# Expert stage's head, the end of attention and the order of FFN's last chunks: work moved between stages, engines and places in their queues

## The chip, the cores and the metric

The kernel runs on one core of a Trainium2 chip, as one program in one launch. The metric is the device time of an execution in microseconds. The kernel before took 1101.15 us (median of 3 runs, 1100.53 to 1102.22). Engines: PE is TensorE (PEld its weight loads), DVE is VectorE, ACT is ScalarE, POOL is GpSimd, SP is SyncE, which issues transfers.

## The reference

Two transformer layers over x of 2 x 1024 tokens with 128 features, all in float32:

```
x = layernorm(x + attention_16_heads(x))
x = layernorm(x + x + 0.5 * (silu(h @ w1 + b1) @ w2 + b2))   # h: x normalised; w1, w2 dequantised
x = layernorm(x + attention_1(x))                            # scores over all 128 features
n = x * rsqrt(mean(x * x) + 1e-8) * norm_weight
p = sigmoid(n @ router_w.T); the two largest of 8, divided by their sum + 1e-6, are the gates
moe = sum over 8 experts: gate_e * (relu(n @ ew1[e] + eb1[e]) @ ew2[e] + eb2[e])
x = layernorm(x + shared_ffn(n) + moe)                       # shared_ffn: the same form, gate 1
```

The inner residual of FFN is its own (the first `x +` belongs to the layer, the second to the FFN). All 8 experts are computed for all tokens.

## The kernel before, in words

There are four stages, and each is a block: no engine enters the next one before all have left the last. `attend_heads` is the first attention (to 717 us), `quantised_ffn` follows (to 760), then `attend_once` (to 851.7) and `mix_experts` (to the end). The 2048 tokens are 16 tiles of 128 (`T`), or 4 chunks (`CK`, `CHUNKS`) of 512 columns. Chunks 0 and 1 are the early ones, 2 and 3 the late ones (`LATE` = 2). Every product that must be exact is three matmuls: operands are split into a high part, rounded to fp32r, and a low part, which is the rest, and hi*lo, lo*hi and hi*hi are added up in a PSUM bank.

Within a stage each engine has its own queue, written out by hand as a Python function per engine; it is worked off in order. Semaphores tie the queues together (`wait_ge`, `then_inc`).

**FFN.** VectorE's queue is at L891-905. `enter` (L851) puts a chunk's normalised tokens in place of X, `leave` (L864) adds the second product of a chunk and sums for the output's layernorm, `finish` (L881) scales the chunk. `leave` waits for `finish` of the chunk before, since there is one set of statistics for all chunks. ScalarE's `out_root` (L823) takes the root between them.

**Second attention, last step.** In step `STEPS` nothing is left but the products with V (`times_v`), four groups. For each, VectorE inverts the denominator (L1229), ScalarE scales the group (L1179) and VectorE puts the output together (L1233), which frees one of the two PSUM banks. Between them stand, for the early chunks, the layernorm's normalising `normalise_tokens` (L1840-1849, at kt 1 and 3, L1238), the turning of chunk 0's tokens on TensorE (L1127), ScalarE's scaling and rounding of it (L1183, L1185), VectorE's low part (L1241) and GpSimd's `normalise_input` for chunks 0 and 1 (L1017, L1852).

**Expert stage.** `over_ffns` (L1328) runs nine FFNs: `ffn(0)` is the shared one, `ffn(1)` to `ffn(8)` are experts 0 to 7, six of them in a hardware loop. An FFN n has 16 tiles (c, f), four chunks by four parts of the hidden layer. TensorE takes turns: `first_product(n, c, f)` (L1414) into one of two banks `bank_h`, then `second_product` of the chunk before (L1432). ScalarE's `rectify` (L1535) empties `bank_h`; `lead` (L1548, L1627) makes the high part on ScalarE (on VectorE for f = 1 and 3 from expert 0 on), GpSimd the low part (L1382; VectorE's `rest`, L1634, for f = 3 from expert 0 on). VectorE's `take` and `add` (L1640, L1651) multiply by the gates and add to `y_sum`. `split_weights` (L1513 on ScalarE, L1620 on VectorE) splits the next expert's weights; `first_product(n, 0, 0)` waits for it (`w_lo_ready`).

The head of that stage is this. TensorE multiplies the late chunks by the output weights (`times_wo`), turns chunk 1's tokens between them (L1490-1493), and in `ffn(0)` turns chunk 2 and 3 after the tiles of chunk 0 and 1; it multiplies by the router after chunk 1 (`ROUTE_AT` = 1, L1486) and turns the gates after chunk 3 (`GATES_AT` = 3). VectorE adds and sums chunks 2 and 3, normalises both, fills `gates[0]` with ones (L1614), then scales and subtracts both (L1615-1618); in `ffn(0)` it chooses the gates (`choose_gates`, L1705), after that makes the low parts of expert 0's weights, and then takes chunks 0 and 1 of the shared FFN. ScalarE's high parts of chunks 2 and 3 (`take_hi`) stand after the last tile of chunk 0 and 1, its sigmoid after chunk 1. GpSimd fills `y_sum` first (L1372), and after `ffn(0)` it has `normalise_input` for chunks 2 and 3. The gates go to memory and back (SyncE, L1350, L1346), and only after them SyncE loads expert 1's weights (L1353).

```python
for c in range(LATE, CHUNKS):        # FFN, VectorE, L896-905
    normalise_ffn(nc, dve, X, fq, c)
leave(0)
finish(0)
enter(2)
enter(3)
for c in range(1, CHUNKS):
    leave(c)
    finish(c)
```

Of the kernel before, what the change touches and what calls it, by code (L numbers as in the profile page):

```python
# [20 lines left out]
P = 128  # L21
CH = 512
# [659 lines left out]
def quantised_ffn(nc, a, persist):  # L682
# [8 lines left out]
    with ExitStack() as ctx:  # L691
# [9 lines left out]
        out_stats, out_mv = sb("ln_out_stats", [P, 4, 6]), sb("ln_out_mean_var", [P, 4, 2])  # L701
        out_std, out_rstd = sb("ln_out_std", [P, 4]), sb("ln_out_rstd", [P, 4])
# [102 lines left out]
        def _(act):  # L805
# [17 lines left out]
            def out_root(c):  # L823
                act.wait_ge(out_moments, c + 1)
                nc.scalar.activation(out_std[:], out_mv[:, :, 1], ACT.Sqrt, bias=eps[:, 2:3]).then_inc(out_rooted, 1)
# [18 lines left out]
        def _(dve):  # L844
# [19 lines left out]
            def leave(c):  # L864
                dve.wait_ge(b2_added, c + 1)
                if c:
                    dve.wait_ge(out_done, c)
                for j in range(4):
                    dve.wait_ge(z_filled, c + 1 + (j if c == CHUNKS - 1 else 0))
                    add_z(c, j)  # L870
                    if j:
                        dve.wait_ge(z_added, 4 * c + j)
                        nc.vector.bn_stats(out_stats[:, j - 1, :], X[:, 4 * c + j - 1, :])
                dve.wait_ge(z_added, 4 * c + 4)
                nc.vector.bn_stats(out_stats[:, 3, :], X[:, 4 * c + 3, :]).then_inc(out_summed, 1)
                dve.wait_ge(out_summed, c + 1)
                for j in range(4):
                    last = nc.vector.bn_aggr(out_mv[:, j, :], out_stats[:, j, :])
                last.then_inc(out_moments, 1)

            def finish(c):  # L881
                dve.wait_ge(out_rooted, c + 1)
                nc.vector.reciprocal(out_rstd[:], out_std[:]).then_inc(out_inverted, 1)
                dve.wait_ge(out_inverted, c + 1)
                for j in range(4):
                    t = 4 * c + j
                    last = nc.vector.tensor_scalar(X[:, t, :], X[:, t, :], out_mv[:, j, 0:1], out_rstd[:, j:j + 1],
# [52 lines left out]
def attend_once(nc, a, persist):  # L940
# [10 lines left out]
    with ExitStack() as ctx:  # L951
# [56 lines left out]
        def _(pool):  # L1008
# [8 lines left out]
            for c in range(EARLY):  # L1017
                normalise_input(nc, pool, X, ln, c)
# [10 lines left out]
        def _(pe):  # L1029
# [97 lines left out]
            def turn_tokens(c):  # L1127

                pe.wait_ge(exp_done, TB * STEPS)
                pe.wait_ge(ln["n_ready"], c + 1)  # L1130
                for j in range(4):
                    last = nc.tensor.transpose(bank_a[c][:, j * P:(j + 1) * P], persist["n_tok"][:, 4 * c + j, :], ident[:])
                last.then_inc(ln["n_turned"], 1)

            for n in range(AHEAD):
                max_scores(n)
            for step in range(STEPS + 1):
                for kt in range(TB):
# [9 lines left out]
                    if step == STEPS and kt == TB - 3:  # L1148
                        turn_tokens(0)

        @block.scalar
        def _(act):
# [16 lines left out]
            for step in range(STEPS + 1):  # L1169
                for kt in range(TB):  # L1170
# [10 lines left out]
                    if step == STEPS and kt == TB - 3:  # L1181
# [731 lines left out]
```

## Time and profile before

| | |
|---|---|
| median of 3 runs | 1101.15 us |
| the profiled execution: its own time / its span | 1102.37 / 1100.6 us |
| TensorE busy, matmuls | 1040.3 us, 95% of the span |
| VectorE busy | 842.6 us, 77% |
| ScalarE busy | 646.9 us, 59% |
| GpSimd busy | 693.1 us, 63% |
| mean granted TensorE clock | 0.972 |
| chain that ended last | PE 15%, DVE 4%, POOL 1%, ACT 1%, issue 1% |

The span is the time from the first to the last instruction; 1.8 us of the execution's own time lie around it. A granted clock of 1.00 is 2.4 GHz, 0.50 is 1.2 GHz; a value between is a stretch with both. A line of a group gives the busy time, and behind it the idle time of the engine just before these instructions and what ended it. A busy TensorE counts matmuls at whichever clock they ran.

### The profile page before, as it was taken

What the parts mean: (1) busy time and instruction counts of PE and PEld (TensorE: products, weight loads), DVE (VectorE), ACT (ScalarE), POOL (GpSimd) and SP (SyncE); (2) the same over time, 40 slices, a digit from 0 to 9 for tenths busy, and PEclk for the clock granted to TensorE, in tenths of its full rate; (3) what the DMA queues carried; (4) which work ended last, traced back from release to release, by engine and by line L of the source; (5) the groups of instructions that cost most, each with busy time, mean ns of one, the idle gap of its engine ahead of it and who ended that gap; (6) DMA issues with size and microseconds to landing.
All of it is one profiled execution on the core that took longest, in us unless ns stands there. A gap on an engine that the chain in (4) does not pass through costs nothing. (4 is left out here: it accounts for less than half of the span.)

```text
span 1100.6 us, 25309 instructions
## 1 busy us (share of the span) xinstructions
PE 1040.3 (95%) x7983; PEld 858.3 (78%) x7983; DVE 842.6 (77%) x1685; ACT 646.9 (59%) x1311; POOL 693.1 (63%) x671
## 2 busy tenths in 40 slices
PE   5899999999999999999999999887998799999996
PEld 4678888888888888888888888655686677777774
DVE  5877877877877877877877877646765589898896
ACT  4555655655655555555555555664344577666774
POOL 4166876876876876876876877511233377777772
PEclk9989999999999999999999999998899799999998
DMA  6243543543543543543543543110000012212111
GB/s 126 49 93 84 104 95 84 105 94 84 106 94 85 106 93 84 106 93 84 107 92 84 108 92 79 45 31 1 0 1 2 18 61 81 72 57 76 58 39 38
DMA packets 57040, 80.08 MB, mean 73 GB/s; under 512 B 25956, under 2 KB 38048, under 8 KB 55968
## 3 DMA queue, kind: packets, MB, share of 16 engines
q1 hardware_dynamic: 54792, 78.97, 31.4%
q10 hardware_dynamic: 2208, 0.59, 0.3%
q8 instruction: 24, 0.39, 0.1%
q14 instruction: 16, 0.13, 0.0%
HBM read 19.43 MB, written 1.11 MB: 19 GB/s over the span
## 5 line engine op out<-in xcount | busy, mean ns | idle before, releaser
L666 POOL TENSOR_TENSOR probs_lo<-probs 128x512 f16<-128x512 f32 x384 | 419.0, 1105 | 199.6 <-ACT probs L470 197.8
L511 DVE TENSOR_REDUCE maxes<-bank_m 128x1 f32<-128x512 f32 x512 | 353.0, 690 | 138.5 <-PE bank_m L301 134.1
L470 ACT ACTIVATE probs<-bank_s 128x512 f32<-128x512 f32 x512 | 297.4, 607 | 264.9 <-PE bank_s L389 264.3
L382 PE MATMUL bank_s<-qa,ka 128*128 128x512 f32 x512 | 226.6, 442 | 7.3 <-ACT probs L470 3.4
L301 PE MATMUL bank_m<-ka,qa 128*128 128x512 f32 x512 | 207.5, 405 | 2.4 <-DMA ka<-tk_lo 2.4
L389 PE MATMUL bank_s<-qb,kb 65*128 65x512 f32 x512 | 206.5, 403 | 1.1 <-DMA qb<-negmax 1.1
L324 PE MATMUL bank_o<-v_now,probs 128*128 128x129 f16 x2048 | 201.9, 221 | 0.3 <-ACT o_parts L436 0.2
L1382 POOL TENSOR_TENSOR hidden_lo<-rectified,hidden_hi 128x512 fp32r<-128x512 f32 x112 | 156.3, 1414 | 67.1 <-ACT hidden_hi L1554 56.9
L324 PEld LDWEIGHTS bank_o<-v_now,probs 128*128 128x128 bf16 x2048 | 176.2, 98 | 21.3 <-issue 20.5
L320 PE MATMUL bank_o<-v_now,probs_lo 128*128 128x65 f16 x2048 | 185.8, 193 | 0.0
L301 PEld LDWEIGHTS bank_m<-ka,qa 128*128 128x128 f32 x512 | 158.7, 310 | 29.1 <-issue 2.6
L320 PEld LDWEIGHTS bank_o<-v_now,probs_lo 128*128 128x128 f16 x2048 | 174.0, 98 | 0.0
L1546 ACT ACTIVATE rectified<-bank_h,e_bias_now 128x512 f32<-128x512 f32 x144 | 99.2, 689 | 60.1 <-PE bank_h L1430 35.6
L382 PEld LDWEIGHTS bank_s<-qa,ka 128*128 128x128 f32 x512 | 97.4, 190 | 41.1 <-ACT probs L470 30.6
L389 PEld LDWEIGHTS bank_s<-qb,kb 65*128 65x128 f32 x512 | 98.0, 191 | 10.3 <-DMA qb<-negmax 1.4
L588 DVE TENSOR_TENSOR probs_lo<-probs 128x512 f16<-128x512 f32 x128 | 102.0, 797 | 3.8 <-ACT probs L470 3.8
L436 ACT ACTIVATE o_parts<-bank_o,rden 128x129 f32<-128x129 f32 x256 | 79.8, 367 | 2.5 <-DVE rden L523 1.4
L1632 DVE CAST hidden_hi<-rectified 128x512 fp32r<-128x512 f32 x64 | 53.0, 828 | 22.5 <-ACT rectified L1546 22.5
L1654 DVE TENSOR_TENSOR y_sum<-y_sum,y_gated 128x512 f32<-128x512 f32 x36 | 52.3, 1452 | 0.1
L1554 ACT CAST hidden_hi<-rectified 128x512 fp32r<-128x512 f32 x80 | 49.0, 613 | 2.6 <-PE bank_y L1447 2.2
L1004 POOL TENSOR_TENSOR probs_lo<-probs 128x512 f16<-128x512 f32 x16 | 17.1, 1073 | 43.6 <-ACT probs L1174 43.6
L641 POOL TENSOR_TENSOR o_pair<-o_parts 128x256 f32<-128x256 f32 x64 | 41.0, 640 | 4.3 <-ACT o_parts L436 4.3
(269 smaller groups left out, 1686.4 us busy)
## 6 DMA issues: line engine op xcount, KB each, us to landing
qa<-tq_hi SPq DMA_DIRECT2D x64, 256.0 KB, 4.1
v_now<-arena SPq DMA_DIRECT2D x32, 260.0 KB, 2.3
ka<-tk_hi SPq DMA_DIRECT2D x32, 256.0 KB, 3.0
ka<-tk_lo SPq DMA_DIRECT2D x32, 256.0 KB, 5.1
kb<-tk_hi SPq DMA_DIRECT2D x32, 256.0 KB, 5.1
qb<-tq_lo SPq DMA_DIRECT2D x32, 256.0 KB, 5.3
gates_on_all<-gate_rows SPq DMA_DIRECT2D x8, 1024.0 KB, 4.7
e_raw<-in_L_ffn_ew_dram SPq DMA_DIRECT2D x16, 256.0 KB, 3.1
```

The lines of the kernel that those rows point to most:

```text
L301: nc.tensor.matmul(bank_m[j % 2][:], qs, ka[h][:, half * CH:(half + 1) * CH], start=True, stop=True).then_inc(m_filled, 1)
L320: low = lambda: nc.tensor.matmul(acc[:, 0:E + 1], probs_lo[:, s % 2, kt, qs], v[:, kt, 0:E + 1], start=False, stop=False, skip_group_check ...
L324: last = nc.tensor.matmul(acc[:, 0:2 * E + 1], hi_of[:, kt, qs, 1], v[:, kt, 0:2 * E + 1], start=(kt == 0), stop=(kt == UNITS - 1))
L382: nc.tensor.matmul(bank_s[u % 2][:], ka[h][:, ks], qa[h][:, qs], start=True, stop=False)
L389: nc.tensor.matmul(bank_s[u % 2][:], kb[h][0:E + 1, ks], qb[h][0:E + 1, qs], start=False, stop=True).then_inc(s_filled, 1)
L436: nc.scalar.activation(out, src[:, 0:P + 1], ACT.Copy, scale=rden[:, qt:qt + 1]).then_inc(o_taken, 1)
L470: nc.scalar.activation(probs[:, c, u, :], bank_s[u % 2][:], ACT.Exp, scale=SCALE).then_inc(exp_done, 1)
L511: nc.vector.tensor_reduce(maxes[:, j // 2, j % 2:j % 2 + 1], bank_m[j % 2][:], AX.X, ALU.max).then_inc(m_reduced, 1)
L588: nc.vector.tensor_tensor(probs_lo[:, c, u, :], p, hi, ALU.subtract).then_inc(lo_dve, 1)
L666: nc.gpsimd.tensor_tensor(probs_lo[:, c, u, :], p, hi, ALU.subtract).then_inc(lo_pool, 1)
L1382: nc.gpsimd.tensor_tensor(h_lo[:, f, :], r[:, f, :], h_hi[:, f, :].bitcast(F32), ALU.subtract).then_inc(lo_pool, 1)
L1546: nc.scalar.activation(r[:, f, :], bank_h[f % 2][:], ACT.Relu, bias=b1_now[:, half, f:f + 1]).then_inc(rectified, 1)
```

## The change

- FFN: statistics of the output's layernorm get a place per chunk; VectorE's order becomes enter 2, enter 3, (leave, finish) 0, (leave, finish) 1, leave 2, leave 3, finish 2, finish 3.
- Second attention: the early chunks' tokens are normalised after the second and the fourth group (kt 3 and 7); turning, scaling and splitting chunk 0 and GpSimd's two `normalise_input` leave the stage.
- Expert stage: both early chunks are turned there, between the products with the output weights; ScalarE scales and rounds them, GpSimd makes their low parts. GpSimd fills `gates[0]` with ones in place of VectorE, and `y_sum` after the tiles of chunk 0.
- VectorE adds, sums and normalises chunk 2, then chunk 3.
- ScalarE's high parts of chunk 2 and 3 come after tiles (1, 1) and (2, 0); router and sigmoid after tile (2, 1).
- VectorE makes the low parts of expert 0's weights ahead of the choice of gates. The gates are turned after chunk 0 of expert 0 (`GATES_AT` = (1, 0): FFN 1, chunk 0), so FFNs 1 and 2 are taken out of the hardware loop.
- `normalise_input` of chunks 0 to 3 stands after chunk 0 and 3 of FFN 1, chunk 2 of FFN 2 and chunk 1 of FFN 7.

```diff
@@ quantised_ffn, VectorE
             def leave(c):
                 dve.wait_ge(b2_added, c + 1)
-                if c:
-                    dve.wait_ge(out_done, c)
...
-            leave(0)
-            finish(0)
-            enter(2)
-            enter(3)
-            for c in range(1, CHUNKS):
+            for c in range(LATE, CHUNKS):
+                enter(c)
+            for c in range(LATE):
                 leave(c)
+                finish(c)
+            for c in range(LATE, CHUNKS):
+                leave(c)
+            for c in range(LATE, CHUNKS):
                 finish(c)
@@ attend_once: GpSimd, TensorE, ScalarE, VectorE
-            for c in range(EARLY):
-                normalise_input(nc, pool, X, ln, c)
...
-                    if step == STEPS and kt == TB - 3:
-                        turn_tokens(0)
...
-                    if step == STEPS and kt == TB - 3:
-                        act.wait_ge(ln["n_turned"], 1)
-                        nc.scalar.activation(nt[:, 0:CH], bank_a[0][:], ACT.Copy, scale=nw).then_inc(ln["nt_ready"], 1)
-                        act.wait_ge(ln["nt_ready"], 1)
-                        nc.scalar.copy(nt_hi[:, 0:CH], nt[:, 0:CH]).then_inc(ln["nt_hi_ready"], 1)
...
-                    if step == STEPS and kt in (1, 3):
-                        normalise_tokens(nc, dve, X, persist["n_tok"], ln, kt // 2)
-            dve.wait_ge(ln["nt_hi_ready"], 1)
-            nc.vector.tensor_tensor(nt_lo[:, 0:CH], nt[:, 0:CH], nt_hi[:, 0:CH].bitcast(F32), ALU.subtract).then_inc(ln["nt_lo_ready"], 1)
+                    if step == STEPS and kt in (3, 7):
+                        normalise_tokens(nc, dve, X, persist["n_tok"], ln, kt // 4)
@@ mix_experts
-        ROUTE_AT, GATES_AT = 1, 3
+        ROUTE_AT, GATES_AT = (2, 1), (1, 0)
+        HI_AT = {(1, 1): 2, (2, 0): 3}
+        INPUT_AT = {(1, 0): 0, (1, 3): 1, (2, 2): 2, (NE - 1, 1): 3}
...
             ffn(0, 0)
-            with eng.Fori(0, NE // 2 - 1) as m:
+            ffn(1, 1, 0)
+            ffn(2, 0, 0)
+            with eng.Fori(1, NE // 2 - 1) as m:
@@ GpSimd
-            nc.gpsimd.memset(y_sum[:], 0.0).then_inc(lane_ready, 1)
+            nc.gpsimd.memset(gates[0][:], 1.0).then_inc(gates_in[0], 16)
+            for c in range(LATE):
+                cs = slice(c * CH, (c + 1) * CH)
+                pool.wait_ge(hi_ready, c + 1)
+                nc.gpsimd.tensor_tensor(nt_lo[:, cs], nt[:, cs], nt_hi[:, cs].bitcast(F32), ALU.subtract).then_inc(lo_ready, 1)
...
-                if first_ffn:
-                    for c in range(LATE, CK):
-                        normalise_input(nc, pool, X, ln, c)
+                    if first_ffn and c == 0:
+                        nc.gpsimd.memset(y_sum[:], 0.0).then_inc(lane_ready, 1)
+                    if isinstance(n, int) and (n, c) in INPUT_AT:
+                        normalise_input(nc, pool, X, ln, INPUT_AT[n, c])
@@ TensorE
+                        if first_ffn and (c, f) == ROUTE_AT:
+                            route()
                     if first_ffn and c + 2 < CK:
                         turn_tokens(c + 2)
-                    if first_ffn and c == ROUTE_AT:
-                        route()
-                    if first_ffn and c == GATES_AT:
+                    if isinstance(n, int) and (n, c) == GATES_AT:
                         turn_gates()
-            times_wo(LATE)
-            turn_tokens(1)
-            for c in range(LATE + 1, CK):
-                times_wo(c)
+            for c in range(LATE):
+                times_wo(LATE + c)
+                turn_tokens(c)
@@ ScalarE
-            act.wait_ge(turned, 2)
-            nc.scalar.activation(nt[:, CH:2 * CH], bank_y[1][:], ACT.Copy, scale=nw).then_inc(nt_ready, 1)
-            take_hi(1)
-            root_of_variance(nc, act, ln, LATE, 1e-8)
+            for c in range(LATE):
+                act.wait_ge(turned, c + 1)
+                nc.scalar.activation(nt[:, c * CH:(c + 1) * CH], bank_y[c][:], ACT.Copy, scale=nw).then_inc(nt_ready, 1)
+                take_hi(c)
+                if c == 0:
+                    root_of_variance(nc, act, ln, LATE, 1e-8)
...
-                            if c < 2 and f == 3:
-                                take_hi(c + 2)
+                            if (c, f) in HI_AT:
+                                take_hi(HI_AT[c, f])
+                            if (c, f) == ROUTE_AT:
+                                act.wait_ge(routed, 1)
+                                nc.scalar.activation(prob[:].rearrange("p t e -> p (t e)"), bank_c[1][:, 0:T * NE],
+                                                     ACT.Sigmoid).then_inc(gated, 1)
@@ VectorE
-            add_and_sum(nc, dve, X, ln, LATE, bank_y[LATE])
-            take_lo(1)
-            add_and_sum(nc, dve, X, ln, LATE + 1, bank_y[LATE + 1])
             for c in range(LATE, CK):
+                add_and_sum(nc, dve, X, ln, c, bank_y[c])
                 normalise_tokens(nc, dve, X, n_tok, ln, c)
-            nc.vector.memset(gates[0][:], 1.0).then_inc(gates_in[0], 16)
...
                 if first_ffn:
+                    split_weights(1, 1)
                     choose_gates()
-                    split_weights(1, 1)
```

## Rows read from the trace of the kernel before

**Rows 1.** Window of an expert's length: us, busy PE, PEld, DVE, ACT, POOL, PEclk, DMA
```profile
920.00:943.00 23.00, 22.62 (x98) 17.91 (x96) 20.35 (x23) 16.13 (x29) 16.95 (x13) 1.00 0.21 69
```

**Rows 2.** TensorE's waits from 850 us on: total us, times, longest us
```profile
PE bank_h L1426 <- ACT rectified L1546: 4.0, 2, 3.7
...
PE bank_h L1426 <- DVE shared_lo L1624: 1.3, 4, 0.4
PE bank_y L1404 <- DVE arena L1847: 1.2, 1, 1.2
PE bank_y L1445 <- POOL hidden_lo L1382: 1.2, 1, 1.2
PE bank_c L1411 <- DVE arena L1617: 0.8, 1, 0.8
```

**Rows 3.** Timeline of FFN's and attention's ends: start us, us, instruction [idle before]
```profile
731.81 3.74 PE L789 MATMUL bank_z<-arena,y 128*128 128x128 f32 x32
...
743.51 3.16 DVE L855 TENSOR_SCALAR x_tokens<-x_tokens,ffn_mv,ffn_rstd 128x128 f32<-128x128 f32 x8
...
754.29 1.06 PE L789 MATMUL bank_b<-arena,y 128*128 128x128 f32 x8
...
758.50 1.11 DVE L887 TENSOR_SCALAR x_tokens<-x_tokens,ln_out_mean_var,ln_out_rstd 128x128 f32<-128x128 f32 x4
...
848.56 0.37 ACT L1179 ACTIVATE o_hi<-bank_p,rden 128x128 f32<-128x128 f32 x1 [2.49 <-DVE rden L1229]
...
850.74 0.69 DVE L1241 TENSOR_TENSOR nt_lo<-arena,nt_hi 128x512 fp32r<-128x512 f32 x1
```

**Rows 4.** The chain of waits, 850 to 960 us: start us, us, piece
```profile
858.78 3.05 DVE arena L1847 x4
...
865.49 1.76 DVE gates_on_all L1614
...
869.89 0.43 PE bank_h L1427
...
875.91 5.16 PE bank_c L1411 x32
...
904.61 0.23 PE bank_y L1447
```

**Rows 5.** Short windows for the clock, columns as in rows 1
```profile
857.00:858.00 1.00, 1.00 (x5) 0.74 (x3) 0.96 (x5) 0.28 (x1) 0.00 (x0) 0.76 0.00 0
...
874.50:875.00 0.50, 0.50 (x5) 0.32 (x3) 0.00 (x0) 0.33 (x1) 0.00 (x0) 0.95 0.00 0
...
878.00:878.50 0.50, 0.50 (x4) 0.50 (x3) 0.00 (x0) 0.00 (x0) 0.00 (x0) 0.50 0.00 0
...
884.50:885.00 0.50, 0.50 (x3) 0.45 (x2) 0.41 (x6) 0.50 (x2) 0.09 (x1) 0.72 0.06 16
```

**Rows 6.** Timeline of the expert stage's head, other engines
```profile
857.72 0.69 ACT L1546 ACTIVATE rectified<-bank_h,e_bias_now 128x512 f32<-128x512 f32 x1 [1.31 <-PE bank_h L1430]
...
858.96 0.68 ACT L1546 ACTIVATE rectified<-bank_h,e_bias_now 128x512 f32<-128x512 f32 x1
...
896.16 0.49 PE L1426 MATMUL bank_h<-nt_hi,e_hi 128*128 128x512 f32 x1
...
897.15 1.49 POOL L1859 TENSOR_TENSOR x_tokens<-x_tokens,ln_attn_mean_var 128x512 f32<-128x512 f32 x1
...
899.45 0.35 SPq L1346 DMA_DIRECT2D gates_on_all<-gate_rows  x1
```

**Rows 7.** Timeline of VectorE, choice of gates and expert 0's low parts
```profile
881.41 1.19 DVE L1717 MAX8 top<-gates 128x8 f32<-128x8 f32 x16 [4.18 <-ACT gates L1574]
...
887.46 1.37 DVE L1730 TENSOR_TENSOR is_first<-is_first,gates 128x128 f32<-128x128 f32 x1
...
891.30 0.25 DVE L1733 RECIPROCAL top_inv<-top_sum 128x16 f32<-128x16 f32 x1
...
892.57 3.47 DVE L1624 TENSOR_TENSOR e_lo<-e_raw,e_hi 128x512 fp32r<-128x512 f32 x2
```

More of the change, by code:

```diff
@@ L700, in quantised_ffn @@
         y = sb("y", [P, 2, NF, CH])
-        out_stats, out_mv = sb("ln_out_stats", [P, 4, 6]), sb("ln_out_mean_var", [P, 4, 2])
-        out_std, out_rstd = sb("ln_out_std", [P, 4]), sb("ln_out_rstd", [P, 4])
+        out_stats, out_mv = sb("ln_out_stats", [P, CHUNKS, 4, 6]), sb("ln_out_mean_var", [P, CHUNKS, 4, 2])
+        out_std, out_rstd = sb("ln_out_std", [P, CHUNKS, 4]), sb("ln_out_rstd", [P, CHUNKS, 4])
         bank_t = [ps(f"bank_t{i}") for i in range(2)]
@@ L872, in leave @@
                         dve.wait_ge(z_added, 4 * c + j)
-                        nc.vector.bn_stats(out_stats[:, j - 1, :], X[:, 4 * c + j - 1, :])
+                        nc.vector.bn_stats(out_stats[:, c, j - 1, :], X[:, 4 * c + j - 1, :])
                 dve.wait_ge(z_added, 4 * c + 4)
-                nc.vector.bn_stats(out_stats[:, 3, :], X[:, 4 * c + 3, :]).then_inc(out_summed, 1)
+                nc.vector.bn_stats(out_stats[:, c, 3, :], X[:, 4 * c + 3, :]).then_inc(out_summed, 1)
                 dve.wait_ge(out_summed, c + 1)
                 for j in range(4):
-                    last = nc.vector.bn_aggr(out_mv[:, j, :], out_stats[:, j, :])
+                    last = nc.vector.bn_aggr(out_mv[:, c, j, :], out_stats[:, c, j, :])
                 last.then_inc(out_moments, 1)
@@ L882, in finish @@
                 dve.wait_ge(out_rooted, c + 1)
-                nc.vector.reciprocal(out_rstd[:], out_std[:]).then_inc(out_inverted, 1)
+                nc.vector.reciprocal(out_rstd[:, c, :], out_std[:, c, :]).then_inc(out_inverted, 1)
                 dve.wait_ge(out_inverted, c + 1)
@@ L886, in finish @@
                     t = 4 * c + j
-                    last = nc.vector.tensor_scalar(X[:, t, :], X[:, t, :], out_mv[:, j, 0:1], out_rstd[:, j:j + 1],
+                    last = nc.vector.tensor_scalar(X[:, t, :], X[:, t, :], out_mv[:, c, j, 0:1], out_rstd[:, c, j:j + 1],
                                                    ALU.subtract, ALU.mult)
@@ L1125, in times_wo @@
                 last.then_inc(ln["y1_filled"], 1)
[L1127 to L1133, printed above, removed]
             for n in range(AHEAD):
@@ L1571, in ffn @@
                             split_weights(n + 1, 1 - half)
-                    if first_ffn and c == ROUTE_AT:
-                        act.wait_ge(routed, 1)
-                        nc.scalar.activation(prob[:].rearrange("p t e -> p (t e)"), bank_c[1][:, 0:T * NE], ACT.Sigmoid).then_inc(gated, 1)
-                    if first_ffn and c == GATES_AT:
+                    if isinstance(n, int) and (n, c) == GATES_AT:
                         for g in range(CK):
```

2 lines of the change are left out of this document (1 added, 1 removed).

## The prediction

> **What bounds the kernel now.** I went from the page to TensorE's waits in the expert stage, from there to the chain of waits, then to short windows for the clock, and last to the timeline of each place that the diff touches. Times called s+ count from the start of the expert stage, which is 851.7 us in this trace; a "product tile" is three matmuls, and a "step" is a first and a second product, six matmuls.
>
> The steady part of the expert stage is bound by TensorE: in a window of 23 us it is busy 22.6, VectorE 20.4, GpSimd 17.0 [rows 1]. The diff does not touch that loop, so it can pay only in the stage's first 45 us and at the ends of the two stages before it. There TensorE waits: 3.7 us for ScalarE's rectifying, 1.2 for the tokens of chunk 2, 0.8 for the scaled tokens ahead of the router, 1.2 for a low part of the hidden values [rows 2]. The chain says where the 3.7 comes from: VectorE normalises chunk 2 in 3.05 us and chunk 3 likewise (four instructions of this kind take 1.11 where GpSimd is still [rows 3]), fills the gates with ones in 1.76, and only then scales chunk 2, on which ScalarE's queue stands; ScalarE cannot rectify what TensorE needs drained [rows 4]. The long idle time costs twice. After it a matmul takes 0.43 us, against 0.23 later [rows 4]. In short windows the clock is at 1.2 GHz until about 874.5, at 2.4 during the transposes and half of the router's 32 matmuls (5.16 us in all [rows 4]), at 1.2 again from 878.0 on, while the router's eight-column matmuls run, and at 2.4 from 884.7 [rows 5]. Expert 0's products begin at 896.16, s+44.5 [rows 6], held by VectorE, which makes the weights' low parts after the whole choice of gates [rows 7].
>
> **1. FFN's order.** Chunks 2 and 3 enter before chunk 0 leaves: eight instructions of 3.16 us [rows 3] move from behind TensorE's last chunks into a wait for its second products. Nothing behind them got later by them, since TensorE ends at 755.35 either way (754.29 plus 1.06) [rows 3]. At the end, chunk 3's additions no longer wait for chunk 2's finish: additions and sums end 1.1 us after TensorE's last matmul, about 756.5, then come two finishes of 0.2 + 1.11 each, so 759.2 instead of 759.61 (758.50 plus 1.11) [rows 3]. Gain 0.4. Bounds: nothing, and 1.3, the whole of chunk 2's finish.
>
> **2. End of attention.** Normalising chunk 0 moves behind the second group of that step, chunk 1 behind the last; turning, scaling, rounding and subtracting chunk 0 leave the stage, as do four GpSimd instructions. Before, ScalarE's third scaling waits 2.49 us for a reciprocal that stands behind chunk 1's normalising, and the subtraction ends at 851.43 (850.74 plus 0.69) [rows 3]. After: third reciprocal behind chunk 0's normalising at about 846.9, last output at 849.05, chunk 1's 0.2 + 1.11 behind it, 850.4. Gain 1.0 to 1.1; I take 1.05. The bound from below is 0.7, the subtraction alone.
>
> **3. Head of the expert stage.** TensorE gets four transposes more (0.9 us at 1.2 GHz). ScalarE scales and rounds two chunks (0.69 + 0.62 each) instead of one before it can rectify. So its first rectifying comes at s+6.9 instead of s+6.0: a cost of 0.9 to 1.3, taken 1.15. GpSimd subtracts both low parts, about 1.3 us each. A gates fill leaves VectorE; that on GpSimd runs in the first 2 us, beside nothing. From then on chunk 0's four tiles are paced by ScalarE, 1.24 us each (858.96 minus 857.72) [rows 6].
>
> Does the 3.7 us wait go? Chunk 2 is normalised by about s+6.3 to 7.5, chunk 3, behind its root on ScalarE, by s+13.1 at GpSimd's pace; the scaled chunk 2 stands at s+13.8; ScalarE now takes its high part between tiles (1,1) and (1,2), at s+14.7, and TensorE asks for it at s+16.6. It goes, and what is late next is nothing by 1 us. Also gone: the 1.2 for chunk 2's tokens and the 0.8 before the router, which now waits behind two steps of chunk 2. The slow stretch from 869.09 to 874.5 then runs fast: 5.4 × (1 - 0.23/0.43) = 2.5. The router at 2.4 GHz takes some 3.7 instead of 5.16 (a row of 32 fp32 matmuls in the stage of FFN took 3.74 [rows 3]; the router's load as many weights): 1.4. The slow stretch from 881.07 to 884.7 gives 1.7. Sum of gains 3.7 + 1.2 + 0.8 + 2.5 + 1.4 + 1.7 = 11.3, less 1.15: 10.15.
>
> But the router stays, and in the profile the clock falls while it runs and stays low for 6.7 us [rows 5]. In the new order it has busy steps on both sides. The cost lies between 0 (no fall) and 3.1 (6.7 us at half rate, by the same factor). I take 2.0, nearer the row. Head: 8.15 gained, expert 0's products at s+33.6 in place of s+44.5, of which 2.4 is the turning of the gates that now comes after chunk 0 of expert 0.
>
> A rule speaks against the eight transposes. In the trace TensorE is busy with transposes and short products at the stage's start, and the clock rises between 857 and 858, 5.6 us after it [rows 5]. The Trainium skill ("TensorE: Matmul & The Clock Gate", Part 4) says that transposes don't count for the clock as other matmuls do. By it, the rise comes after chunk 0's first tiles, and since ScalarE paces those, the sum changes by 0.3 to 1 us only.
>
> **4. Choice of gates.** The low parts of expert 0's weights (3.47 us beside GpSimd) go ahead of the choice; that serves TensorE, which would need them at s+33.6 [rows 7]. The choice starts when the sigmoid stands, s+24.4 instead of s+29.7. It took 11.2 us (881.41 to 892.57). Its large steps each took one GpSimd instruction's time (1.37) beside GpSimd, the reciprocal 0.25 [rows 7]. GpSimd is busier beside it now, until it waits itself for VectorE's part of expert 0. Bounds 9 and 15.5; I take 12.5, so the choice ends at s+37. TensorE asks for it at s+39.2. Then VectorE has two take-and-add pairs (2.9), and its share of expert 0's first chunk; it delivers the last low part at about s+45, TensorE wants it at s+46. That is the thinnest margin: 0.3 to charge. The wait of 1.2 on GpSimd in expert 0 [rows 2], made by two normalisings in front of it, goes. With 0.2 for gates and weights loads, see the second rival: net gain 0.7.
>
> **5. Input normalisings.** These were two pairs at the end of attention, hidden, and two pairs before expert 0. Now they stand one by one inside experts 0, 0, 1 and 6. A pair is 2.1 us alone, 3.0 beside VectorE (1.49 for one) [rows 6]. GpSimd's idle time is 6.05 in 23 us, 1.5 per chunk [rows 1]. So each pair is late by 0.6 to 1.5 us, and the low part of the weights, for which TensorE already waits (1.3 in four times) [rows 2], is stretched too. The first pair hides behind the turning of the gates. The other three cost 0 to 1.5 each; I take 2.8 together. Filling y_sum behind chunk 0's tiles delays GpSimd by 1.8 where its results are wanted 2 us later: nothing.
>
> **Sum.** -0.4 - 1.05 - 8.15 - 0.7 + 2.8 = -7.5. The profiled execution took 1102.4 (span 1100.6), 1.2 more than the median 1101.15. On it 1094.9, on the median 1093.6; I say 1093.5.
>
> **Rivals.** *VectorE bounds expert 0.* If the choice takes 15.5 us because GpSimd never pauses beside it, it ends at s+40; TensorE waits 0.8 at the gates and some 2.5 to 3 at the last low part. For it: every large step took a GpSimd instruction's time. Against: GpSimd needs VectorE's high parts from expert 0 on, and must pause. Gain 4: 1097. Chance 0.14. *Loads bound expert 0.* SyncE sends expert 1's weights only after the gates' rows have gone to memory and the first gates load is issued; that issue came 3.3 us after expert 0's start (899.45) [rows 6]; it would now come at 10.7, with 5 us to land, while ScalarE asks at about 15. Stall 1 to 2.5 us: 1095. Chance 0.12. *More than forecast:* the clock does not fall after the router and the normalisings hide: 7.5 + 2.0 + 2.0, 1089.7. Chance 0.14. *Slower.* VectorE's 16 searches for the eight largest and 32 index instructions have only run with GpSimd idle in this trace (881.41 on) [rows 7]. Beside it, if each waited out one GpSimd instruction of 1.4 us, the choice would grow by some 40 us and TensorE would stand at the gates: about 1120. It turns the sign from a growth of about 10 us. Against it is the reciprocal, also with one input, which kept 0.25 beside GpSimd. Chance 0.03. The Trainium skill ("SBUF — State Buffer", Who interferes with whom) says that a VectorE instruction with at most one input in SBUF, outside its two-port modes, does not contend with GpSimd. By it this rival is void, as the reciprocal's row has it. *The change does not do what it says*: the stall only moves to chunk 3, whose high part needs VectorE's subtraction of chunk 2, the scaling and ScalarE in turn; with a second idle time and clock fall the head gives 2 instead of 8: 1100. Chance 0.07.
>
> **Numbers.** The forecast itself has 0.50. A difference of under 0.2% (2.2 us) can't be told from none here. The range takes in the forecast's bounds and the first three rivals, 1089.0 to 1098.3. Faster 0.89 (all but 0.11), same 0.07, slower 0.04.
>
> **What the profile would show.** TensorE's wait on rectifying near s+14 gone; first products at 2.4 GHz; one low-clock stretch around the router; expert 0's products at s+32 to s+36; VectorE's choice 11 to 14 us long, ahead of TensorE's request; GpSimd's normalisings followed by waits of TensorE for low parts of about 1 us. Wrong if TensorE waits over 2 us for the chosen gates, for a weights load, or in chunk 2.

## The result, and the profile of the changed kernel

| | before | after |
|---|---|---|
| median of all runs | 1101.14 us | 1097.89 us |
| lowest, highest | 1096.58, 1104.70 | 1092.42, 1100.37 |
| profiled execution, its span | 1102.37, 1100.6 | 1099.89, 1098.1 |
| mean granted clock in it | 0.972 | 0.977 |

The changed kernel takes 0.9971 of the time before, 95% interval 0.9957 to 0.9984: 3.2 us faster, 1.8 to 4.7. The forecast was 7.6 us faster. Direction and range hold; the size is less than half.

TensorE's waits of the changed kernel from 848 us on: total us, times, longest us.

```profile
PE bank_h L1416 <- ACT rectified L1537: 3.1, 3, 2.5
PE bank_y L1386 <- PEq L951: 2.6, 1, 2.6
PE bank_h L1416 <- DVE e_lo L1613: 2.5, 3, 1.9
PE bank_h L1416 <- DVE shared_lo L1613: 1.3, 3, 0.5
PE bank_y L1435 <- POOL hidden_lo L1371: 1.0, 2, 0.5
```

They answer to [rows 2]. The 1.2 for chunk 2's tokens and the 0.8 ahead of the router are gone. A wait on ScalarE's rectifying still heads the list, but it is another one: it stands at 904 us, inside expert 0, and not at the head. The 2.6 on PEq is the start of the stage itself (3.6 before). Of the 2.5 us for the weights' low parts most is new (0.8 before, by the same view of the kernel before).

I then took the first product of each FFN from the timeline. The shared FFN starts the stage; the columns are how long each lasts until the next one's first product.

| us | shared | e0 | e1 | e2 | e3 | e4 | e5 | e6 |
|---|---|---|---|---|---|---|---|---|
| before | 40.16 | 24.60 | 22.85 | 22.87 | 22.90 | 22.90 | 22.82 | 22.75 |
| after | 29.67 | 29.52 | 25.40 | 24.43 | 22.86 | 22.89 | 22.80 | 24.22 |

Expert 0's products begin 44.4 us after the stage's start before and 32.7 after (883.33 minus 850.67): the head gives 11.8. Experts 0, 1, 2 and 6 give back 4.92 + 2.55 + 1.56 + 1.47 = 10.5, of which the gates' turning, now inside expert 0, was foreseen at 2.4. Between TensorE's first matmuls of the stages, the attention stage is 2.6 shorter (91.57 to 88.93), the FFN stage 1.0 longer (42.52 to 43.54) and the code ahead of it, which the diff does not touch, 0.5 longer: 11.8 - 10.5 + 2.6 - 1.0 - 0.5 = 2.4, where the two profiled executions differ by 2.5. Not all of it belongs to the change. The new attention stage took 88.1 to 89.0 us in eleven traces and the old one 90.0 to 91.6 in three, so single traces differ by as much as 1.6 without a difference in that code. The same holds for the head: at the stage's start the clock stood at 1.2 GHz for 3.4 us in four of the eleven traces with the new head, and in the three of them that have the router's slow stretch too, expert 0's products begin at 33.6. In this trace the start ran at 2.4 GHz, and they begin at 32.7. The steady part is the same: 22.63 us busy in 23, as in [rows 1]. The window is one of expert 3, columns us, busy PE, PEld, DVE, ACT, POOL, clock, DMA:

```profile
962.00:985.00 23.00, 22.63 (x98) 17.91 (x96) 20.34 (x23) 16.15 (x29) 16.91 (x13) 1.00 0.22 69
```

What fills expert 0: the timeline of SyncE, ScalarE and TensorE there.

```profile
892.63 0.32 SPq L1335 DMA_DIRECT2D gate_rows<-comb_t  x1
...
895.11 0.35 SPq L1331 DMA_DIRECT2D gates_on_all<-gate_rows  x1
...
895.98 0.43 SPq L1327 DMA_DIRECT2D e_raw<-in_L_ffn_ew_dram  x1
...
902.28 1.14 ACT L1509 CAST shared_hi<-e_raw 128x512 fp32r<-128x512 f32 x2 [3.31 <-DMA e_raw<-in_L_ffn_ew_dram]
...
904.25 0.51 PE L1416 MATMUL bank_h<-nt_hi,e_hi 128*128 128x512 f32 x1 [2.54 <-ACT rectified L1537]
```

Expert 1's weights are asked for only at 895.98, behind the gates' rows and the first gates load; they land 6.3 us later. ScalarE has been standing at their split for 3.31 us with the rectifying behind it in its queue, and TensorE stands for 2.54. Then the clock is at 1.2 GHz for 3.4 us: eight matmuls of 0.43 us each in place of 0.23, some 1.5 us more.

What fills experts 1 and 2: the timeline of GpSimd, VectorE and TensorE at the end of expert 1.

```profile
932.96 1.50 POOL L1848 TENSOR_TENSOR x_tokens<-x_tokens,ln_attn_mean_var 128x512 f32<-128x512 f32 x1
...
933.47 1.53 DVE L1626 TENSOR_TENSOR hidden_lo<-rectified,hidden_hi 128x512 fp32r<-128x512 f32 x1
...
934.92 3.19 DVE L1613 TENSOR_TENSOR e_lo<-e_raw,e_hi 128x512 fp32r<-128x512 f32 x2
...
938.25 0.49 PE L1416 MATMUL bank_h<-nt_hi,e_hi 128*128 128x512 f32 x1 [1.95 <-DVE e_lo L1613]
```

The input's normalising of chunk 2 stands just ahead of and beside VectorE's split of the next expert's weights. VectorE's subtraction takes 1.53 beside it, the split 3.19, and TensorE waits 1.95 us; the chain then has matmuls of 0.43 us until 942. The wait counts into expert 1's 25.40 us, the slow matmuls are what makes expert 2's 24.43 out of 22.9.

The head did what was forecast. VectorE's choice, which answers to [rows 7], and the router in the chain, which answers to [rows 4]:

```profile
869.39 3.00 DVE L1613 TENSOR_TENSOR e_lo<-e_raw,e_hi 128x512 fp32r<-128x512 f32 x2 [0.35 <-ACT e_hi L1509]
...
883.36 0.98 DVE L1723 TENSOR_TENSOR comb_by_token<-is_first,top_inv 128x128 f32<-128x128 f32 x1
```

```profile
868.38 4.60 PE bank_c L1401 x32
```

The clock by windows, which answer to [rows 5]: in the stage's head one slow stretch is left, around the router.

```profile
870.00:871.00 1.00, 1.00 (x9) 1.00 (x8) 1.00 (x2) 0.95 (x3) 1.00 (x2) 0.73 0.00 0
871.00:872.00 1.00, 1.00 (x7) 1.00 (x6) 1.00 (x1) 1.00 (x1) 1.00 (x2) 0.50 0.00 0
...
877.00:878.00 1.00, 1.00 (x6) 0.77 (x5) 0.97 (x2) 0.70 (x2) 0.81 (x1) 0.85 0.00 0
878.00:879.00 1.00, 1.00 (x6) 0.81 (x5) 0.90 (x4) 0.97 (x2) 0.32 (x1) 1.00 0.02 8
```

### The profile page after: what moved, and what is told of

It is laid out like the page before. It is cut to its first block and busy times, and to the rows that moved or that the text cites. A ratio compares the mean times of both kernels' runs of the same rounds, so it can differ in the third digit from the quotient of the medians.

```text
span 1098.1 us, 25143 instructions
## 1 busy us (share of the span) xinstructions
PE 1040.5 (95%) x7983; PEld 855.6 (78%) x7983; DVE 841.6 (77%) x1682; ACT 648.3 (59%) x1311; POOL 701.7 (64%) x674
```

## The experiments

Theories. **A**: expert 1's weights are queued behind the gates, and the shorter head has made that late. **B**: GpSimd's four pairs that normalise the input cost more inside the experts than forecast. Rivals: **C**, the gates turned inside expert 0; **D**, the clock's falls are chance. The kernels below build on the changed kernel unless said otherwise. Times are medians; the ratio to the kernel before has its 95% interval.

**e1_early_load**

```diff
             load(0)
+            sp.wait_ge(w_lo_ready, 1)
+            load(1)
             sp.wait_ge(comb_t_ready, CK)
...
             load_gates(0, 1)
-            sp.wait_ge(w_lo_ready, 1)
-            load(1)
```

> The changed kernel, with SyncE's load of expert 1's weights put ahead of its wait for the turned gates and of the gates' store and load. Theory A (expert 1's weights are queued behind the gates, so ScalarE's split in expert 0's FFN waits for them 3.3 us, TensorE idles 2.5 to 2.9 us and its clock falls once, about 1.8 us more): the load is issued near the start of the router, some 20 us earlier, ScalarE's wait for e_raw is gone, expert 0's FFN takes 24.6 to 25.4 us instead of 29.5, and the kernel is 4 to 5 us faster than the changed kernel's 1097.9, so 1093 to 1094 us. Theory B (GpSimd's normalising of the input and its port are what stretches the experts): the wait goes, but expert 0's FFN still takes 28 us or more, and the kernel gains under 1.5 us (1096.5 to 1098). Theory C (the gates turned inside expert 0's FFN): as B, under 1.5 us.

Measured: 1096.41 us, ratio 0.9961 (0.9947 to 0.9975). The load goes out at 871.95 instead of 895.98:

```profile
871.95 0.43 SPq L1327 DMA_DIRECT2D e_raw<-in_L_ffn_ew_dram  x1
...
894.90 1.13 ACT L1509 CAST shared_hi<-e_raw 128x512 fp32r<-128x512 f32 x2
```

ScalarE's split no longer waits, and expert 0 takes 25.51 us instead of 29.52. That is A for expert 0, and it refutes C as the cause of this stall: the gates are still turned there. But the kernel gains only 1.5 us in the medians, outside A's 4 to 5 and at the edge of B's bound, and its interval overlaps the changed kernel's (0.9957 to 0.9984), so the runs alone do not show a gain. The two traces' experts 0 to 6 differ by 3.5. Expert 1 takes 0.6 more, with the same wait of 2.0 for e_lo.

**e2_no_normalise** and **e3_early_no_norm** (the second with e1's edit as well)

```diff
-        INPUT_AT = {(1, 0): 0, (1, 3): 1, (2, 2): 2, (NE - 1, 1): 3}
+        INPUT_AT = {}
...
-                pe.wait_ge(ln["done"], 2 * CK)
```

> The changed kernel without GpSimd's four pairs that normalise the input, and without TensorE's wait for them at the end; the output lacks that normalisation of the layer's input. Theory B: experts 1, 2 and 6 fall from 25.4, 24.4 and 24.2 us to 22.9 each, 5.4 us in all, and expert 0 is unchanged by theory A: 1092 to 1093.5 us. Theory A alone with free normalising: under 1 us gained (1097 to 1098). Theory D (clock falls are chance, not tied to these pairs): the long experts of the one trace appear elsewhere or not at all, and the time stays within 1.5 us of the changed kernel's.

> Both edits together: expert 1's weights loaded ahead of the gates, and no normalising of the input. If A and B are separate and both right, the gains add: 4.5 + 5.2 us under the changed kernel, 1087.5 to 1089.5 us, and every expert's FFN takes 22.8 to 23.5 us except the first (24 to 25, gates turned in it). If both edits cure the same stall (a split of expert 1's weights that comes late for either cause), the sum is less than the parts: 1091 to 1093 us.

Measured: 1094.56, ratio 0.9943 (0.9920 to 0.9966), and 1090.44, ratio 0.9905 (0.9885 to 0.9926). The first gains less than B's 1092 to 1093.5, the second lies between its two ranges. Without the pairs experts 1, 2 and 6 take 22.68, 22.90 and 22.74 us in e2_no_normalise, while expert 0 keeps its stall (3.04 us, and 29.83 in all). The four medians stand in a square, and behind each the time of experts 0 to 6 in the trace:

| | weights behind gates | weights first |
|---|---|---|
| pairs in the experts | 1097.89, 172.1 | 1096.41, 168.7 |
| no pairs | 1094.56, 166.7 | 1090.44, 162.5 |

The pairs cost 6.0 us where the load is early, and the load's place costs 4.1 where the pairs are gone. By the medians each alone gives 2.6 less. The traces show an overlap of 0.7 only: the load's place costs 3.5 with the pairs and 4.2 without, the pairs 5.4 and 6.1. With intervals of about 2 us on either side the medians do not tell these apart, and the 2.6 is not shown. The runs alone show the pairs' cost; that of the load's place rests on the traces. D falls for the stalls: in these four traces they sit where the pair or the late load is, and nowhere without it. It does not fall for the slow matmuls behind them, see e8_low_behind_choice.

**e4_ffn_alone**: the kernel before with the first layer's FFN of the changed kernel.

```diff
-            leave(0)
-            finish(0)
-            enter(2)
-            enter(3)
-            for c in range(1, CHUNKS):
+            for c in range(LATE, CHUNKS):
+                enter(c)
+            for c in range(LATE):
                 leave(c)
                 finish(c)
...
```

> The kernel before with the new order of VectorE's work in the first layer's FFN alone, and nothing else of the change. The prediction gave it -0.4 us. By the two traces the FFN stage took 42.5 us before and 43.5 us after, of which one stretch at the lower clock in the traced execution explains about 1.7 us, so the order itself would be worth -0.4 to -0.7 us: 1100.4 to 1100.8 us. Rival (the new order starves TensorE early in the stage and the lower clock is its doing): slower by 0.5 to 1.5 us, 1101.6 to 1102.6 us, with the low clock in the same place.

Measured: 1101.01 us, ratio 1.0002 (0.9986 to 1.0018): no difference that runs can tell. The traces can. From FFN's first matmul to VectorE's first instruction of attention the old order took 42.56 us in the kernel before and 44.21 in e10_before_early_load; the new order 41.87 to 41.88 us in six traces and 43.51 to 43.57 in six others. In 44.21 and in the 43.5s the clock stands at 1.2 GHz for 3.4 us near 731, and in the others it does not. So the order gives 0.7 us in either case, on two traces of the old one, and the clock falls there under either order (one of two traces, six of twelve). What decides it was not tried. The comparison of the two first traces had a fall in one of them only, 1.7 us that are not part of the change.

**e5_no_mean** (with e1's edit)

```diff
-    if c:
-        pool.wait_ge(ln["done"], 2 * c)
-    nc.gpsimd.tensor_tensor(x, x, wide(ln["mv"][:, c, :, 0]), ALU.subtract).then_inc(ln["done"], 1)
-    pool.wait_ge(ln["done"], 2 * c + 1)
     nc.gpsimd.tensor_tensor(x, x, wide(ln["rstd"][:, c, 0, :]), ALU.mult).then_inc(ln["done"], 1)
```

> Expert 1's weights loaded ahead of the gates, as in e1_early_load, and of each GpSimd pair that normalises the input only the scaling, one instruction instead of two (the final normalisation takes each token's mean away again, so the output does not change). Theory B (each pair is paid for by the time that GpSimd and the port are taken): the cost of the pairs, 6.0 us between e1_early_load (1096.4) and e3_early_no_norm (1090.4), halves: 1093 to 1094 us, with experts 0, 1, 2 and 6 at 24.9, 24, 23 and 23.2 us. Theory B2 (a threshold: half a pair fits into the slack that GpSimd has per chunk, 1.5 us): nearly all of it goes, 1090.5 to 1091.5 us.

Measured: 1092.71 us, ratio 0.9916 (0.9894 to 0.9938): 3.7 of the 6.0 are gone with half of the work, which lies between B's range and B2's. Expert 1 still takes 24.83, with a wait of 1.1 for e_lo behind the one instruction that is left at that place, and expert 6 23.56.

**e6_scalar_scale** (with e1's edit)

```diff
-        INPUT_AT = {(1, 0): 0, (1, 3): 1, (2, 2): 2, (NE - 1, 1): 3}
+        INPUT_AT = {}
...
+            def scale_input(c, j):
+                act.wait_ge(ln["n_ready"], c + 1)
+                x = X[:, 4 * c + j, :]
+                nc.scalar.activation(x, x, ACT.Copy, scale=ln["rstd"][:, c, 0, j:j + 1]).then_inc(ln["done"], 1)
...
+                        if isinstance(n, int) and n == 2:
+                            scale_input(c, f)
```

> As e5_no_mean, but ScalarE does the scaling, sixteen instructions of 128x128, one behind each tile of expert 1, and GpSimd does nothing of it. ScalarE is busy 1.4 us in 2 there and has no part in the wait for low parts. Theory B (the cost is GpSimd's time and what VectorE loses beside it): the time of e3_early_no_norm, 1090 to 1091.5 us. Rival (any work put into the experts lengthens them, since ScalarE also paces TensorE through rectifying): expert 1 takes 24 to 26 us and the kernel 1092 to 1094 us.

Measured: 1089.59 us, ratio 0.9903 (0.9882 to 0.9924), the time without any normalising. Expert 1, with all sixteen instructions in it, takes 23.09. ScalarE's time was free to 0.2 us here; GpSimd's and VectorE's was not.

**e7_pair2_later** (with e1's edit)

```diff
-        INPUT_AT = {(1, 0): 0, (1, 3): 1, (2, 2): 2, (NE - 1, 1): 3}
+        INPUT_AT = {(1, 0): 0, (1, 3): 1, (2, 3): 2, (NE - 1, 1): 3}
```

> As e1_early_load, with the normalising of chunk 2 behind GpSimd's low parts of chunk 3 of expert 1 instead of chunk 2. Theory B3 (this pair costs most because it stands beside VectorE's split of the next expert's weights, for which TensorE then waits 2 us with a clock fall behind it): the wait of 1.9 us for e_lo goes, a wait of about 1 us for hidden_lo takes its place, expert 1 and 2 together fall from 50.4 to about 47 us, and the kernel gains 2 to 3 us on e1_early_load: 1093.5 to 1094.5 us. If place does not matter: 1095.5 to 1097 us.

Measured: 1093.92 us, ratio 0.9935 (0.9910 to 0.9960), 2.5 us under e1_early_load. The split is back to 2.38 us and the wait to 0.29:

```profile
929.18 2.38 DVE L1613 TENSOR_TENSOR e_lo<-e_raw,e_hi 128x512 fp32r<-128x512 f32 x2
...
931.70 0.49 PE L1416 MATMUL bank_h<-nt_hi,e_hi 128*128 128x512 f32 x1 [0.29 <-DVE e_lo L1613]
...
934.67 1.49 POOL L1848 TENSOR_TENSOR x_tokens<-x_tokens,ln_attn_mean_var 128x512 f32<-128x512 f32 x1
```

Experts 1 and 2 take 48.7 us together instead of 50.4, not the 47 expected: the pair now makes TensorE wait on hidden_lo (1.9 us in three times). In the medians this place costs 2.5, over a third of the 6.0, but the two intervals overlap. In the traces it is 1.7, and 1.5 of it are the slow matmuls in expert 2: where they stay away behind the same wait, in e8_low_behind_choice below, experts 1 and 2 take 48.9.

**e8_low_behind_choice**

```diff
-                    split_weights(1, 1)
                     choose_gates()
+                    split_weights(1, 1)
```

> The changed kernel with VectorE's low parts of expert 0's weights behind the choice of gates again, nothing else undone. The prediction says that the choice would end at s+31 to s+34 then, the low parts at s+34 to s+37, and TensorE wants them at s+30 to s+32 (the changed kernel's expert 0 starts at s+32.7, of which 2.4 or more is a slow stretch), so that it waits 3 to 6 us and the clock falls behind it: 1101 to 1105 us. Rival (TensorE would wait for the gates at tile (1,0) anyway, and the load behind the gates hides a late start): the wait replaces the 3 us wait for expert 1's weights, and the kernel loses under 2 us, 1098 to 1100.

Measured: 1100.98 us, ratio 1.0002 (0.9989 to 1.0016), 3.1 us over the changed kernel. This one part undone takes away the whole gain. TensorE waits up to 3.2 us for e_lo, the first FFN takes 32.94 us instead of 29.67, and the stall for the load (2.4) is still there behind it, so the rival's "replaces" is wrong. The time lies just under the range of 1101 to 1105.

This trace shows one thing more. Behind the stall for the load and behind the wait of 1.95 for e_lo the clock stayed at 2.4 GHz, where it fell in the changed kernel's trace:

```profile
910.23 0.50 PE L1416 MATMUL bank_h<-nt_hi,e_hi 128*128 128x512 f32 x1 [2.43 <-ACT rectified L1537]
...
944.16 0.49 PE L1416 MATMUL bank_h<-nt_hi,e_hi 128*128 128x512 f32 x1 [1.95 <-DVE e_lo L1613]
```

```profile
911.00:912.00 1.00, 1.00 (x6) 0.80 (x5) 0.31 (x2) 1.00 (x3) 1.00 (x1) 1.00 0.00 0
...
945.00:946.00 1.00, 1.00 (x6) 0.82 (x5) 1.00 (x3) 0.14 (x1) 1.00 (x2) 1.00 0.78 164
```

Expert 2 takes 22.89 us here and 24.43 and 24.40 in the two traces with the fall, so one fall costs 1.5. Among the waits of 1.9 us or more inside the FFNs of all traces with the new head, the clock fell within 1 us of the wait's end at five of seven, and stayed at 2.4 GHz at two. The stall is made by the load or the pair; whether the slow matmuls come behind it differs from trace to trace, and what decides it was not tried.

**e9_pairs_ahead** (with e1's edit; the pairs about where the kernel before had them)

```diff
-        INPUT_AT = {(1, 0): 0, (1, 3): 1, (2, 2): 2, (NE - 1, 1): 3}
+        INPUT_AT = {(0, 3): (2, 3)}
...
                     make_lo(nc.gpsimd, pool, step, kt, lo_pool)
+            normalise_input(nc, pool, X, ln, 0)
...
             nc.gpsimd.memset(gates[0][:], 1.0).then_inc(gates_in[0], 16)
+            normalise_input(nc, pool, X, ln, 1)
```

> As e1_early_load, but GpSimd's pairs stand ahead of the experts as in the kernel before: chunk 0 at the end of attention, chunk 1 at the start of the expert stage, chunks 2 and 3 behind the first FFN's last low part. Theory B: experts 1, 2 and 6 fall to 22.8 to 22.9 us each, which takes off 6 us of e1_early_load's 1096.4; expert 0 pays 1 to 1.5 us for its two pairs by TensorE's wait for hidden_lo (1.2 before), and chunk 1's pair beside VectorE's first normalisings up to 1 us: 1091.5 to 1093 us. If the first FFN has no room for them (VectorE makes the choice there, beside GpSimd), 1094 to 1097 us.

Measured: 1091.58 us, ratio 0.9923 (0.9899 to 0.9946), 4.8 us under e1_early_load. Experts 1, 2 and 6 take 22.82, 22.89 and 22.71; expert 0 takes 26.01, which is 0.5 more than without pairs.

**e10_before_early_load**: e1's edit in the kernel before.

> The kernel before with only SyncE's order changed: expert 1's weights ahead of its wait for the turned gates. In the kernel before ScalarE had no wait for e_raw in expert 0, since the gates are turned ahead of expert 0's products: the load had slack, and its order is worth nothing, 1100.5 to 1101.8 us. So the wait for the load is made by the shorter head. Rival (the gates' store and load sit behind the weights then, and VectorE's first gated take waits): 0.5 to 2 us slower.

Measured: 1101.81 us, ratio 1.0018 (0.9997 to 1.0038); expert 0 takes 24.59 as before. The load had slack there: its lateness is a product of the shorter head. The small loss by the rival is not told from none.

**e11_router_in_four** (e6_scalar_scale and this)

```diff
-        ROUTE_AT, GATES_AT = (2, 1), (1, 0)
+        ROUTE_AT, GATES_AT = ((1, 3), (2, 0), (2, 1), (2, 2)), (1, 0)
...
-                pe.wait_ge(nt_ready, CK)
-                for t in range(T):
+                pe.wait_ge(nt_ready, c + 1)
+                for t in range(4 * c, 4 * c + 4):
...
```

> As e6_scalar_scale (1089.6), with the router's product in four groups of four token tiles, each behind one step of the first FFN (tiles (1,3), (2,0), (2,1), (2,2)), instead of all sixteen behind (2,1). If the clock falls around the router because of a long run of eight-column matmuls (in seven traces of such kernels it fell in five, at 869 to 872, and the first FFN then took 29.2 to 29.7 us or more, and 26.5 in the others): it no longer falls, the first FFN takes 26.5 to 27.5 us, the spread of the runs narrows, and the median falls by 1 to 2 us, to 1087.5 to 1088.6. If the fall has another cause: it stays, 29 to 30 us, and the time is that of e6_scalar_scale within 1 us.

Measured: 1086.44 us (1085.27 to 1088.03), ratio 0.9878 (0.9851 to 0.9904), 3.2 us under e6_scalar_scale and more than the 1 to 2 expected; the two intervals overlap. (The expectation's count is one short: there were eight such traces by then, with five falls; with e9_pairs_ahead it is six of nine.) The clock stays at 2.4 GHz through the router, and the first FFN takes 25.90 us. The third group, and windows around the last (columns as above):

```profile
868.95 0.95 PE L1401 MATMUL bank_c<-moe_small,arena 128*128 128x8 f32 x8
```

```profile
868.00:870.00 2.00, 2.00 (x14) 1.80 (x13) 1.90 (x2) 1.97 (x7) 2.00 (x2) 1.00 0.00 0
870.00:872.00 2.00, 2.00 (x14) 1.74 (x13) 2.00 (x2) 1.73 (x3) 1.81 (x2) 1.00 0.00 0
872.00:874.00 2.00, 2.00 (x11) 1.66 (x11) 0.93 (x5) 1.97 (x4) 1.73 (x2) 1.00 0.05 18
```

One caution: e6_scalar_scale's own trace had no fall either, and its first FFN took 26.53. That the fall is gone for good rests on two traces (this and the next, 26.35), on the spread of the runs, 2.8 us against 8.0, and on the medians.

**e12_tokens_early** (e11_router_in_four and this)

```diff
-                    if step == STEPS and kt in (3, 7):
-                        normalise_tokens(nc, dve, X, persist["n_tok"], ln, kt // 4)
+                    if step == STEPS and kt in (1, 3):
+                        normalise_tokens(nc, dve, X, persist["n_tok"], ln, kt // 2)
```

> As e11_router_in_four (1086.4), with VectorE's normalising of chunks 0 and 1 at the end of attention put back behind the first and the second scaling, where the kernel before had it, and nothing else undone. The prediction gave 1.0 to 1.1 us for the whole move. From ScalarE's first o_hi of the last step to the start of the expert stage (its first copy of the biases) it took 8.1 us before and 6.3 after, 1.8 less, the turned chunk 0 included. If VectorE's order is what counts (reciprocals behind 1.1 us of normalising each): this stretch takes 7.0 to 8.1 us again, and the kernel is 0.7 to 1.8 us slower, 1087.1 to 1088.2 us. If the removed turning, scaling and subtraction of chunk 0 gave it: the stretch stays at 6.3 to 6.7 us, and the time within 0.5 us.

Measured: 1085.04 us, ratio 0.9867 (0.9846 to 0.9889), not slower than e11_router_in_four; its 1.4 us less, on four runs, is not told from none, and the two intervals overlap for most of their length. The stretch from ScalarE's first o_hi of the last step to the next stage's first copy is 6.29 us, against 6.28 there and 8.13 in the kernel before. In e12_tokens_early:

```profile
841.48 0.34 ACT L1167 ACTIVATE o_hi<-bank_p,rden 128x128 f32<-128x128 f32 x1
...
847.77 0.19 ACT L1499 COPY e_bias_now<-moe_small 128x1 f32<-128x1 f32 x1 [0.77 <-PEq L951]
```

VectorE's order moves 0.8 us from one side of TensorE's last matmul to the other: from the start of that matmul to the stage's it is 2.03 us here, 2.83 with the change's order, and 3.86 before.

## Why the prediction was half right

**FFN's order**, forecast 0.4, measured 0.7 by fourteen traces, two of them with the old order. Right, though no run can tell it.

**End of attention**, forecast 1.05, measured 1.85 (8.13 to 6.28 us). The size is of the right order, the reason is not: the prediction put it down to the third reciprocal coming out from behind a normalising. e12_tokens_early puts that order back and loses nothing. The gain is the turning, scaling and subtraction of chunk 0, which the prediction had as its lower bound at 0.7.

**Head**, forecast expert 0's products at s+33.6, measured s+32.7. The wait of 3.7 us went, as did the 1.2 and the 0.8; the first products run at 2.4 GHz. Chunk 3 made no new stall, and "does not do what it says" falls. The cost of 1.15 for the stage's start did not come: ScalarE's first rectifying is at s+5.0, not s+6.9, and at s+5.8 to 5.9 in the four traces in which the clock stood at 1.2 GHz there. This outweighs the 1 us by which the router's fall cost more than forecast, and a part of it is luck. The late rise of the clock that the prediction priced at 0.3 to 1 us is not seen here: the clock stood at 2.4 GHz from the stage's start in seven of the eleven traces with the new head. (The prediction's own terms, 8.15 and 2.4, leave 0.35 of its s+33.6 unexplained.) The router's fall, forecast as 2.0 us, costs 2.7 to 3.2 when it comes (first FFN 29.2 to 29.7 us against 26.5), and in three of nine traces it did not. The low parts ahead of the choice are worth 3.1 us by themselves, even with the load's stall behind them.

**Choice of gates**, forecast 12.5 us, ended at s+33.7 instead of s+37, 11.0 long; it never bound expert 0. TensorE's wait at the turning of the gates was 0.9. The rival in which searches wait for GpSimd falls too, and its price did not follow from its own numbers: 48 instructions of 1.4 us are 67, not 40, and a growth of 40 with the sign turning at 10 gives some 1131, not 1120. In e1_early_load GpSimd was busy beside them for most of the time, and sixteen MAX8 took 1.19 us, as in [rows 7] with GpSimd idle:

```profile
869.28 3.42 POOL L1371 TENSOR_TENSOR hidden_lo<-rectified,hidden_hi 128x512 fp32r<-128x512 f32 x2
871.55 1.19 DVE L1706 MAX8 top<-gates 128x8 f32<-128x8 f32 x16
873.31 4.10 POOL L1371 TENSOR_TENSOR hidden_lo<-rectified,hidden_hi 128x512 fp32r<-128x512 f32 x3 [0.61 <-ACT hidden_hi L1545]
```

By the rule of the Trainium skill that the prediction named ("SBUF — State Buffer", Who interferes with whom), a VectorE instruction with at most one input in SBUF, outside the two-port modes, does not contend with GpSimd; the trace agrees for MAX8 at 1.19.

**The first step that failed** is the end of part 4, "With 0.2 for gates and weights loads ...: net gain 0.7". The load's lateness was seen and kept as a rival at 0.12. By its own numbers, issue at 10.7 and 5 us to land against ScalarE at 15, it was 0.7 late and so the forecast, not the rival. One of its signs of being wrong, a wait of over 2 us for a weights load, came. Measured from expert 0's start: issue at 12.7, landing at 18.9, ScalarE at 15.6. And the rival stopped at the stall. It named 1 to 2.5 us, and the stall is 2.54, but the clock fell behind it and took some 1.5 more: 4.0 in the traces (29.52 against 25.51), 1.5 or 4.1 in the medians, with and without the pairs. The prediction had used that very effect as a gain at the head ("The long idle time costs twice") and did not charge it here.

**The second** is the 2.8 of part 5. The pairs cost 6.0 us by the medians and 6.1 by the traces. The pair at (1,0) costs nothing, as forecast. The one at (1,3) costs 1.5 (expert 1 takes 24.33 in e7_pair2_later and 22.83 in e3_early_no_norm), the one at (7,1) 1.5 (expert 6), both at the upper end of the "0 to 1.5 each" of which the 2.8 took less than two thirds. The one at (2,2) costs 1.7 in expert 1 (26.01 against 24.33) and 1.5 in expert 2 by the clock. The prediction says that the weights' low parts are "stretched too" and gives that no price of its own: VectorE's subtraction goes from 0.68 to 1.53 us and the split from 2.38 to 3.19, which together make the wait of 1.95, and the clock fell behind it in two of three traces.

With both repaired the forecast can be compared with its own sum. Without the 2.8 and the 0.2 it was a gain of 10.5 us, and e3_early_no_norm gained 10.9. That the two are so near is in part luck, since several terms above are off in both directions. "More than forecast" at 1089.7 was within reach, but only with the load moved and the pairs off GpSimd (e6_scalar_scale, 1089.59).

## What to carry to other kernels

When a stage's head gets shorter, list every transfer that was issued behind something in it, and work out issue, landing and demand in the new times; if the three do not fit, that is the forecast. Charge each new idle time of TensorE as the wait, and put a price with a chance on the slow matmuls behind it (here 1.5 us, behind five of seven waits of 1.9 us or more). Here helper work on GpSimd cost most beside VectorE's two-input work that TensorE waited for (the split, 3.19 us against 2.38); first ask whether it is needed at all (here a later normalisation takes the mean away again) and whether ScalarE has the time.

The best version here, e12_tokens_early, takes 1085.0 us, 15.7 less than the kernel before it was run against. It differs from the changed kernel in four things: weights first, scaling on ScalarE without the mean, the router in four, and the old order of VectorE at attention's end, the last of which is worth nothing that can be told.

## What was not expected of the hardware

A busy TensorE can lose its clock. During 32 matmuls of eight columns in a row (3.63 us at 2.4 GHz, 4.40 to 4.76 with a fall) with full-size products on both sides, the granted clock fell to 1.2 GHz in six of nine traces and stayed there for 6.8 us. With the same matmuls in four groups of 0.95 us between products it fell in neither of two.

The clock fell or did not fall over the same code from one trace to the next: in the first layer's FFN in six of twelve traces with its new order, worth 1.7 us each time, and behind the wait of 1.95 us for e_lo in two of three. Two single traces can therefore differ by several us without any cause in the change, and a stage should be compared among traces in which the clock did the same.
